# Rotated state of the coupled networks: multiplied by TensorE in every cycle, or carried along by VectorE

## The reference, cut to what matters

```python
def _twist(x):
    o_r, o_i, p_r, p_i = jnp.split(x, 4, axis=-1)
    return jnp.concatenate([p_r, -p_i, -o_r, o_i], axis=-1)

gf = _global_net(mean of x over the tokens)            # one number per sequence
out = x
for _ in range(3):                                     # NUM_CYCLES
    tf = _coupling_net(out, ...)                       # 128 -> 128 -> 64 -> 32 -> 1, gelu between, sigmoid
    combined = 0.7 * gf + 0.3 * tf
    coupling = 0.1 + adaptive_range * (combined - 0.5) * 2.0
    out = out + coupling * _twist(out)
```

## Time and profile before

| | us |
|---|---|
| median of three runs (1410.41, 1412.20, 1422.61) | 1412.2 |
| the profiled execution | 1404.83 |
| its span | 1403.1 |
| TensorE / VectorE / ScalarE / GpSimd busy | 1331.0 / 1159.2 / 1048.9 / 166.7 |
| stage A, from its first w1 to the last w4 | 15.5 to 65.9 |
| stage C, from the second cycle's first w1 to the last w4 | 530.0 to 561.5 |

### The profile page before, as it was taken

How to read it: one execution, slowest core, us unless ns; L and a number is a source line. 1 busy time by engine, 2 the same in 40 slices (tenths; PEclk the granted TensorE clock), 3 DMA queues, 4 the chain that set the end, 5 groups by cost and what they waited for, 6 DMA issues and landing times.

```text
span 1403.1 us, 30189 instructions
## 1 busy us (share of the span) xinstructions
PE 1331.0 (95%) x11933; PEld 481.5 (34%) x11996; DVE 1159.2 (83%) x1532; ACT 1048.9 (75%) x2057; POOL 166.7 (12%) x446
## 2 busy tenths in 40 slices
PE   8988999999999999999799999999999999999899
PEld 4243333332333452534223333332333333333633
DVE  5668889999998166655799999999999999994464
ACT  3547788998999534334289999999999999999231
POOL 9224221211111000001100000000000000000000
PEclk9989999999999999999689999999999999999999
DMA  4042220300000000000402000000000000000000
GB/s 103 1 113 58 38 28 16 47 5 12 4 4 4 11 1 0 1 0 23 134 22 75 4 4 11 4 4 4 12 4 4 3 3 12 4 4 4 11 0 30
DMA packets 35197, 28.81 MB, mean 21 GB/s; under 512 B 16336, under 2 KB 31664, under 8 KB 35056
## 3 DMA queue, kind: packets, MB, share of 16 engines
q1 hardware_dynamic: 35056, 26.88, 8.3%
HBM read 17.03 MB, written 9.70 MB: 19 GB/s over the span
## 4 chain that ended last, share of the span: by engine, by line
DVE 49%; PE 42%; ACT 4%; issue 2%; DMA 1%; SPq 1%; POOL 0%; DVEq 0%; POOLq 0%; ACTq 0%
DVE m_blockmax L1226 45%; PE ps L1121 8%; PE ps L1066 5%; PE ps L1102 4%; PE ps L578 3%; PE ps L589 3%; PE ps L579 2%; ACT m_prob L1203 2%; PE ps L249 2%; PE ps L330 2%; PE ps L236 1%; PE ps L352 1%; PE ps L242 1%; PE ps L1157 1%; DMA ba_sums<-m_pv 1%
## 5 line engine op out<-in xcount | busy, mean ns | idle before, releaser
L1226 DVE TENSOR_REDUCE m_blockmax<-ps 128x2 f32<-128x1024 f32 (+1 forms) x768 | 880.3, 1207 | 26.0 <-PE ps L1066 19.8
L1203 ACT ACTIVATE m_prob<-ps 128x512 f32<-128x512 f32 (+3 forms) x1664 | 843.9, 576 | 40.3 <-PE ps L1102 25.9
L1066 PE MATMUL ps<-m_k_all,m_q_all 64*128 64x512 bf16 (+3 forms) x1664 | 320.3, 383 | 23.2 <-DVE m_blockmax L1226 19.8
L1102 PE MATMUL ps<-m_q_max,m_k_all 64*128 64x512 bf16 (+3 forms) x1664 | 338.6, 367 | 0.5
L1125 PE MATMUL ps<-m_prob,m_v_op 128*16 128x256 f32 x4096 | 321.0, 385 | 0.2
L1066 PEld LDWEIGHTS ps<-m_k_all,m_q_all 64*128 64x128 bf16 x1664 | 79.7, 93 | 350.1 <-DVE m_blockmax L1226 186.2
L1121 PE MATMUL ps<-m_prob,m_v_op 128*16 128x256 f32 (+3 forms) x2560 | 179.3, 352 | 1.7 <-ACT m_pv L1186 0.9
L1102 PEld LDWEIGHTS ps<-m_q_max,m_k_all 64*128 64x128 bf16 x1664 | 144.1, 94 | 94.6 <-ACT m_prob L1203 52.1
L1125 PEld LDWEIGHTS ps<-m_prob,m_v_op 128*16 128x16 f32 x4096 | 67.2, 94 | 133.3 <-issue 101.3
L1250 POOL CAST m_maxparts<-m_negmax 128x8 bf16<-128x8 f32 x64 | 14.1, 220 | 734.0 <-DVE m_negmax L1234 729.3
L1194 ACT ACTIVATE m_q_max<-ps 128x512 bf16<-128x512 f32 x64 | 38.2, 597 | 56.9 <-PE ps L1088 56.6
(11 more groups left out here) (212 smaller groups left out, 1055.2 us busy)
## 6 DMA issues: line engine op xcount, KB each, us to landing
ba_parts<-m_part SPq DMA_DIRECT2D x8, 384.0 KB, 3.3
ea_parts<-m_part SPq DMA_DIRECT2D x8, 384.0 KB, 2.6
m_k_all<-ea_parts SPq DMA_DIRECT2D x84, 32.0 KB
m_q_all<-ea_parts SPq DMA_DIRECT2D x84, 32.0 KB
m_k_all<-ba_parts SPq DMA_DIRECT2D x36, 64.0 KB
m_q_all<-ba_parts SPq DMA_DIRECT2D x36, 64.0 KB
ba_sums<-m_pv SPq DMA_DIRECT2D x128, 9.0 KB
ea_sums<-m_pv SPq DMA_DIRECT2D x128, 9.0 KB
```

The source lines that it names most:

```text
L1066: mm = pe.matmul(ps[:, MX + 2 * (u % 2) + j, 0:width], q_all[head, pair, q0:q0 + TW], k_all[head, pair, CW * kc:CW * kc + width], start=Tr ...
L1102: pe.matmul(ps[:, e % ST, q0:CW], k_all[head, pair, TW * i:TW * i + TW], q_max[m % 2][head, q0:CW], start=True, stop=True).then_inc(self.s ...
L1203: nc.scalar.activation(prob[:, (2 * t + j) % NP, q0:CW], ps[:, e % ST, q0:CW], ACT.Exp, scale=SCALE)\
L1226: nc.vector.tensor_reduce(blockmax[:, m % plan.AHEAD, qt, :, kc], ps[:, MX + 2 * (u % 2):MX + 2 * (u % 2) + 2, 0:width], AX.X, ALU.max)\
```

## The change

The rotated state is no longer made by TensorE in the second and third cycle. If t is the rotated state and a the coupling, then new state = state + a * t, and new rotated state = t + a * twist(t) = t - a * state. So VectorE carries both along. The state now alternates between two buffers, since the old one is still read after the new one is made. The update works on a group of two chunks at a time: scale the tanh in place to a = c1 * th + c0 (2 instructions), ahead = a * t (2), new state = old + ahead (2), back = a * old (2), and t - back (2); in the first cycle t is read from PSUM, later from SBUF. In the third cycle the last four are left out and the two additions to `x` stand in their place. The tanh of the next cycle writes where a lies, and now waits for `back`. `dve_constant` is gone. After the third cycle the first centring of the next norm (chunk 0) goes ahead of the update of chunks 2 and 3, which was split around it before.

```diff
+    def state(self, s):
+        return self.xn if (s - self.start) % 2 == 0 else self.xn2
...
-            pe.matmul(ps[:, c, :], k["cn_w1"][:, :], chunk(xn, c), start=True, stop=True).then_inc(self.w1_done, 1)
+            pe.matmul(ps[:, c, :], k["cn_w1"][:, :], chunk(self.state(s), c), start=True, stop=True).then_inc(self.w1_done, 1)
...
-            twist(0)
-            twist(1)
+            if s == self.start:
+                twist(0)
+                twist(1)
...
-            twist(2)
-            twist(3)
+            if s == self.start:
+                twist(2)
+                twist(3)
...
-                act.wait_ge(self.step_ready, NC * (s - 1) + c + 1)
+                act.wait_ge(self.back_ready, self.backs(s - 1) + c + 1)
...
+    def dve_update(self, dve, s, g):
+
+        nc, pair = self.nc, (2 * g, 2 * g + 1)
+        old, new, last = self.state(s), self.state(s + 1), s == self.end - 1
+        first = s == self.start
+        for c in pair:
+            dve.wait_ge(self.th_ready, NC * s + c + 1)
+            nc.vector.tensor_scalar(chunk(self.th, c), chunk(self.th, c), self.c1[:, 0:1], self.c0[:, 0:1], ALU.mult, ALU.add)\
+                .then_inc(self.scaled, 1)
+        for c in pair:
+            dve.wait_ge(self.scaled, NC * s + c + 1)
+            if first:
+                dve.wait_ge(self.tw_done, NC * self.use + c + 1)
+            else:
+                dve.wait_ge(self.turned_ready, self.backs(s - 1) + c + 1)
+            turned = self.ps[:, NC + c, :] if first else chunk(self.turned, c)
+            nc.vector.tensor_tensor(self.part[:, c % 2, :], chunk(self.th, c), turned, ALU.mult).then_inc(self.ahead, 1)
+        for c in pair:
+            dve.wait_ge(self.ahead, NC * s + c + 1)
+            nc.vector.tensor_tensor(chunk(new, c), chunk(old, c), self.part[:, c % 2, :], ALU.add).then_inc(self.updated, 1)
+        if last:
...
+            return
+        for c in pair:
+            nc.vector.tensor_tensor(self.back[:, c % 2, :], chunk(self.th, c), chunk(old, c), ALU.mult).then_inc(self.back_ready, 1)
+        for c in pair:
+            dve.wait_ge(self.back_ready, self.backs(s) + c + 1)
+            turned = self.ps[:, NC + c, :] if first else chunk(self.turned, c)
+            nc.vector.tensor_tensor(chunk(self.turned, c), turned, self.back[:, c % 2, :], ALU.subtract).then_inc(self.turned_ready, 1)
...
             if s > self.start:
-                self.dve_update(dve, s - 1, 2)
-                self.dve_update(dve, s - 1, 3)
-            self.dve_constant(dve, s, 0)
-            self.dve_constant(dve, s, 1)
+                self.dve_update(dve, s - 1, 1)
             self.dve_update(dve, s, 0)
-            self.dve_update(dve, s, 1)
-            self.dve_constant(dve, s, 2)
-            self.dve_constant(dve, s, 3)
...
                 def ffn_end(ffn, ln, bank):
-                    ffn.dve_update(dve, ffn.end - 1, 2)
                     norm.dve_centre(dve, ln, 0, x, bank)
-                    ffn.dve_update(dve, ffn.end - 1, 3)
+                    ffn.dve_update(dve, ffn.end - 1, 1)
```

More of the change, by code:

```diff
@@ L295, in __init__ @@
         self.h1, self.h2, self.h3 = k["h1"], k["h2"], k["h3"]
-        self.th, self.base, self.step = k["th"], k["base"], k["step"]
+        self.th, self.xn2, self.turned = k["th"], k["xn2"], k["turned"]
+        self.part, self.back = k["ahead"], k["back"]
         self.total = n.sb("total", [P, NC], fp32)
@@ L306, in __init__ @@
             self.w4_done, self.th_ready, self.tw_done = n.sem("w4_done"), n.sem("th_ready"), n.sem("tw_done")
-            self.base_ready, self.step_ready, self.updated = n.sem("base_ready"), n.sem("step_ready"), n.sem("updated")
+            self.scaled, self.ahead, self.updated = n.sem("scaled"), n.sem("ahead"), n.sem("updated")
+            self.back_ready, self.turned_ready = n.sem("back_ready"), n.sem("turned_ready")
         else:
@@ L313, in __init__ @@
             self.w4_done, self.th_ready, self.tw_done = earlier.w4_done, earlier.th_ready, earlier.tw_done
-            self.base_ready, self.step_ready, self.updated = earlier.base_ready, earlier.step_ready, earlier.updated
+            self.scaled, self.ahead, self.updated = earlier.scaled, earlier.ahead, earlier.updated
+            self.back_ready, self.turned_ready = earlier.back_ready, earlier.turned_ready
         self.use = 0 if earlier is None else 1
@@ L477, in dve_total @@
         self.nc.vector.tensor_reduce(self.total[:, c:c + 1], chunk(self.xn, c), AX.X, ALU.add).then_inc(self.summed, 1)
[L479 to L496, removed]
@@ new lines, in backs @@
+    def backs(self, s):
+        return NC * (s - self.use)
+    def dve_update(self, dve, s, g):
[19 more added lines that the diff above has]
+            for c in pair:
+                dve.wait_ge(self.updated, NC * s + c + 1)
+                nc.vector.scalar_tensor_tensor(out=chunk(self.x, c), in0=chunk(new, c), scalar=0.5, in1=chunk(self.x, c),
+                                               op0=ALU.mult, op1=ALU.add).then_inc(self.x_done, 1)
+            return
+        for c in pair:
+            nc.vector.tensor_tensor(self.back[:, c % 2, :], chunk(self.th, c), chunk(old, c), ALU.mult).then_inc(self.back_ready, 1)
+        for c in pair:
+            dve.wait_ge(self.back_ready, self.backs(s) + c + 1)
+            turned = self.ps[:, NC + c, :] if first else chunk(self.turned, c)
+            nc.vector.tensor_tensor(chunk(self.turned, c), turned, self.back[:, c % 2, :], ALU.subtract).then_inc(self.turned_ready, 1)
@@ L1364, in macaron @@
         k["prob"] = prob[:, :].rearrange("p (b n) -> p b n", b=12)
-        k["th"], k["base"], k["step"] = (prob[:, N * b:N * b + N] for b in range(3))
+        k["th"], k["xn2"], k["turned"] = (prob[:, N * b:N * b + N] for b in range(3))
         words = part[:, :].bitcast(fp32)
@@ L1368, in macaron @@
         k["h3"] = words[:, N + 2 * CW:N + 3 * CW]
+        k["ahead"], k["back"] = (words[:, N + at * CW:N + (at + 2) * CW].rearrange("p (g n) -> p g n", g=2) for at in (3, 5))
         k["q_max"] = [n.sb(f"q_max{a}", [P, CW], bf16) for a in range(2)]
```

## The result

The changed kernel takes 1443.92 us (median of four runs, 1436.09 to 1446.59), the kernel before, in the same session, 1412.40. The ratio is **1.020**, 95% interval 1.017 to 1.024: slower by 31.5 us by the medians, by 29 us by the ratio. The prediction said 1415.1, at most 1427. The profiled execution took 1442.7 against 1404.83, 37.9 more.

What follows compares the result with a forecast made beforehand. It took TensorE as the bound before, and afterwards the loop through VectorE's longer answer. Per block 0.77 + 0.66 = 1.4, two blocks +2.9 us on 1412.2 gives 1415.1 us, range 1407 to 1427.

Steps and rivals of the forecast that it cites:

- That is all the slack there is: Coupled-network loop: w1 starts 0.44 and 0.40 us late, so the loop becomes the bound after some 0.84 us.
- The sum at full clock: Two blocks and the norms behind: +0.77 and +0.66 us each, +2.9 in all; chance 0.47 for 1413 to 1417.
- Behind that the lists are the same: Norm behind each block: after the first reciprocal, +0.66 us late, the instruction lists are unchanged.
- The scaling: VectorE's new one-source 128x512 instruction in the update: 0.48 us, 0.38 from one to the next.
- Rival 1, the exclusion: Stage A's first scaling waits 5.4 us for GpSimd's fill, plus 3 at half clock: +11.3, 1423.5 us; chance 0.32.
- no row shows VectorE waiting for a fill: Argument against VectorE's scaling being held up by GpSimd's fill in stage A, a rival given chance 0.32.
- Rival 2, the clock: TensorE's clock falls inside the blocks, its share of a turn being 65%: one block +16 us, 1431; chance 0.10.
- no wait is over 3 us: Blocks: argument against a clock fall, as nearly all matmuls are 512 columns wide and TensorE's waits stay short.
- What a fall costs: Inside the blocks: a turn's 8 us of TensorE on the path doubles; one block at half clock costs +16 us.
- the longer answer: VectorE's answer in the loop grows by 1.3 us against 0.4 of slack: 1.58 us more per turn, +0.77 per block.
- the later norm: Norm behind each block: first reciprocal 9.73 us after the last w4 instead of 9.07, +0.66.

Runs made afterwards that it cites:

- e5: The kernel before with the twist matmuls of the second and third cycle left out, VectorE's instructions unchanged, state not the reference's: 1416.64 us, 1.0005 of before.
- e9: The kernel before with two sums and two one-source scalings on unread tiles added to VectorE beside GpSimd's first fill: 1426.04 us, one run.
- e1: The changed kernel with GpSimd's two fills of k_all moved until after stage A's last addition to x: 1426.65 us, 1.010 of before.
- e2: The changed kernel with TensorE still multiplying the 16 removed twists in their old places, unread: 1430.25 us, 1.014 of before.
- e8: The changed kernel with the scaling as a two-source instruction and the 16 twists multiplied unread, fills unmoved: 1428.56 us, 1.010 of before.
- e6: The changed kernel with the scaling written as a two-source instruction (scalar_tensor_tensor), fills unmoved: 1442.77 us, 1.020 of before.
- e4: Control: the kernel before with GpSimd's two fills of k_all moved until after stage A: 1410.80 us, 1.001 of before.
- e3: The changed kernel with GpSimd's fills moved after stage A and the 16 twists multiplied unread: 1423.46 us, 1.009 of before.
- e7: The changed kernel with late fills, unread twists, and group 1's last update split by chunk around chunk 0's centring: 1420.21 us, 1.004 of before.

## Why the prediction was wrong, point by point

- **"That is all the slack there is": wrong, and without effect on the time.** There was none. The windows that showed TensorE full showed it filled: e5 takes 3.8 us of work a turn out and the turn stays 13.96.
- **The sum at full clock: right.** The turn was forecast at 15.57 and is 15.54; the pause at 2.8 and is 2.75; the last way at 4.96 and is 4.91 (586.45 to 591.36). Stage C is 2.4 us longer than before. Of this its third w1 pair at half clock explains 3.59 - 1.98 = 1.6; the rest is 0.8, the forecast +0.77. The first reciprocal came 10.0 after the last w4 where 9.73 was forecast, at PEclk 0.92. "Behind that the lists are the same" was right of the lists and wrong of the time: the fourth reciprocal came 2.3 us later than before instead of 0.66, at PEclk 0.90.
- **The scaling: a little off.** 0.48 was forecast, it takes 0.546, and 0.45 from one to the next where 0.38 was taken. The pair costs 0.1 more each time. By the figures of the Trainium skill (VectorE: DVE Perf Modes, "The perf-mode tier table") the estimate was 0.42; the trace has 0.546, which is under the 0.68 of a two-tensor instruction but not half of it.
- **Rival 1, the exclusion: it happened, and bigger.** The first scaling waited until 37.2, as the rival said, and then the sums waited for the selects. Together w1 is 6.7 us late instead of the 5.4 of the rival. I gave it 0.32 because "no row shows VectorE waiting for a fill". None could: before the change no scaling or copy of that size runs beside one. The one-source instructions that do, the sums over 512 columns (`TENSOR_REDUCE`, L477) beside the fill L195, take their usual 0.68 us, so the exclusion is one of the scaling and not of every one-source instruction. The row that did bear on it, the select of 0.922 us, I read rightly as a possible wait. The Trainium skill (SBUF — State Buffer, "Who interferes with whom") has both halves: an instruction in a two-port mode and any GpSimd instruction exclude each other, and one with two sources in SBUF is excluded only by a GpSimd instruction that reads. Both are what the trace shows here: scalings of 5.78 and 7.23 us beside the fills (e9), sums of 0.69 us beside a fill and of 1.9 us beside the selects.
- **Rival 2, the clock: this is the step that failed.** It stood at 0.10, and for stage A or C alone. The step was "no wait is over 3 us", from which it followed that nothing would fall. The pause of 8.23 us in stage A broke it outright, since rivals 1 and 2 are not independent: one made the pause on which the other fed. And pauses under 3 us were enough without it: in stage A e1 has none over 2.76 and ran at 0.79, and e5 has none over 1.7 and ran at 0.88. In the norm, which the step left out, the prediction's own numbers hold a longer one: the means of chunks 0 and 1 start at 1.09 and take 1.98, and x of chunk 2 is ready at 6.77, so TensorE had to pause for some 3.7 us; in stage C it was 3.85, and half clock followed. Adding TensorE work that nobody reads won 13.7 us (e2 against after) and 14.2 (e8 against e6), which no explanation by a longer answer or by the exclusion gives.
- **What a fall costs** I had priced only inside the blocks. It goes on behind them: the norm after stage A ran at 0.72 and took 20.52 instead of 15.10.

The sum of the profiled execution, then: of +37.9, blocks and norms hold 28.0. Of that, 6.7 is the exclusion and about 3, by the prediction's terms, the longer answer and the later norm; the remaining 18 or so is the clock, some 12 of it in the blocks and 6 in the norms. The prediction's sum had this term at nothing. The 5.1 and 4.6 in the unchanged stages go with a clock of 0.97 against 0.98 and 0.96 against 0.97, but such differences stand between executions of any two of these kernels (stage B took 446 to 457 us in these profiles), so I don't count them as caused.

**Still open.** At which pause the clock falls is not settled by these runs: of three pauses of 2.7 to 2.8 in stage C one was followed by half clock and two were not, in e6 it fell behind one of 1.95, and in e4, with the old lists, behind 1.59 and 0.33. What the profiles do separate is the loop behind a block's first pair of w1: with the matmuls in place (before, e2, e3, e4, e7, e8, e9) it kept full clock in all 14 blocks, without them (after, e1, e5, e6) it lost it in 7 of 8. Of e3's 12.6 us over before in the profiled executions the blocks hold 3.4 and the norms 4.3; the other 5 lie in stages that the change doesn't touch, and whether they are caused by it is open.

## What to carry to other kernels

An engine that is busy 14.03 of 14.06 us may be filled rather than bound: before you take work from it, follow the loop once through the other engines and ask when its next input would be there. Work that you take from TensorE comes back as pauses, and pauses may cost more in clock than the work did in time; the cheapest trial is to leave the matmuls in, unread. Follow the loop to its end, too: an instruction moved ahead of an update makes TensorE wait for that update. And when a change brings a one-source instruction to VectorE, look up what GpSimd does in that very stretch, and price the stall together with what follows it.

## What the runs showed of the hardware

- A one-source 128x512 single-precision scaling on VectorE and GpSimd's 3x8192 fill do not run together: the scaling waits out the whole fill, 5.78 and 7.23 us instead of 0.546 (e9), 5.32 in the changed kernel. The same arithmetic as a two-source instruction takes 0.75 beside the same fill (e6; one of 0.96 stood beside a select).
- Two-source sums in SBUF were held up by GpSimd's selects (1.9 us instead of 0.684) and not by its fills (0.69, e9). GpSimd's own fill of 128x1024 right behind took 1.12 us beside the changed kernel's scaling and 1.11 in e9, instead of 0.96.
- TensorE's clock fell behind pauses of 1.95 us (the w1 pair of 2.69 at 34.84 in e6), 2.75 and 3.04, and not behind each pause of such a length. Behind the pause of 3.4 to 4.3 us in the norm, which the moved centring makes, there was half clock in all 12 norms of the six kernels that have it (after, e1, e2, e3, e6, e8). Matmuls that nobody reads, put into the pauses, kept it up in the loop: e3 does 30.7 us of work in a block of 35.65 at 1.00, while e6, without them, is busy for 30.3 us in a block of 42.22 at 0.80, since its fewer matmuls take longer.
